# Linear attention and a routed MLP on one core: score products contracted over 32 rows of the key tile, two quarters of the heads in turn

## The reference

```python
qkv = x @ w_attn
q, k, v = jnp.split(qkv, 3, axis=-1)          # after elu+1 on q and k
def step(carry, qkv_t):
    S, z = carry
    qt, kt, vt = qkv_t
    S = S + kt[..., :, None] * vt[..., None, :]
    z = z + kt
    num = jnp.einsum('bhi,bhij->bhj', qt, S)
    den = jnp.sum(qt * z, axis=-1, keepdims=True)
    return ((S, z), num / (den + EPS))
```

## Time and profile before

| what | before |
|---|---|
| time, median of 3 runs (lowest, highest) | 357.5 us (355.8, 362.76) |
| profiled execution, first to last instruction | 339.4 us |
| PE busy | 285.0 us, 84% of the span |
| DVE busy | 241.9 us, 71% |
| ACT busy | 152.0 us, 45% |
| POOL busy | 124.8 us, 37% |
| mean granted TensorE clock | 0.934 |

### The profile page before, as it was taken

One profiled execution on the slowest core, in us unless ns is written; L12 is line 12 of the kernel. 1 busy time (PEld: TensorE's weight loads), 2 busy tenths in 40 slices (PEclk: granted clock), 3 DMA queues, 4 the chain that ended last, 5 costly groups with the idle time before them and its releaser, 6 DMA issues.

```text
span 339.4 us, 10754 instructions
## 1 busy us (share of the span) xinstructions
PE 285.0 (84%) x3847; PEld 245.5 (72%) x3847; DVE 241.9 (71%) x842; ACT 152.0 (45%) x301; POOL 124.8 (37%) x142
## 2 busy tenths in 40 slices
PE   1777989999999999999999998942129999999980
PEld 1446678688688788787787887742119999999980
DVE  4974557778778778778687787663735888988880
ACT  3378491780871871861952830000023444444430
POOL 8979000303503404305305205232311546545662
PEclk9997999999999999999999999785558999999995
DMA  7990000001000001001001001000252334333410
GB/s 212 319 302 5 3 2 2 2 3 35 34 4 37 27 0 48 16 0 63 1 0 64 0 0 66 2 34 33 82 162 70 108 90 117 93 95 97 113 38 0
DMA packets 16906, 20.19 MB, mean 59 GB/s; under 512 B 2747, under 2 KB 13117, under 8 KB 16882
## 3 DMA queue, kind: packets, MB, share of 16 engines
q1 hardware_dynamic: 13040, 12.50, 13.1%
q0 software_dynamic: 2832, 6.57, 5.6%
q10 hardware_dynamic: 1010, 0.81, 0.8%
HBM read 12.22 MB, written 8.10 MB: 60 GB/s over the span
## 4 chain that ended last, share of the span: by engine, by line
PE 63%; DVE 15%; issue 6%; ACT 4%; POOL 3%; DMA 3%; DVEq 2%; SPq 1%; POOLq 0%; ACTq 0%
PE bank L1001 18%; PE bank L1013 5%; PE bank L1138 5%; PE bank L1147 4%; PE bank L1033 4%; PE bank L1020 4%; PE bank L956 3%; DVE k_q L885 3%; PE bank L1062 3%; PE bank L979 2%; PE bank L971 2%; ACT h_t L432 2%; POOL sorted_rows L374 2%; PE bank L962 2%; PE bank L1047 2%
## 5 line engine op out<-in xcount | busy, mean ns | idle before, releaser
L374 POOL DMA_INDIRECT sorted_rows<-row_buf,slot_i x32 | 31.6, 987 | 119.7 <-DVE slot_i L777 112.4
L1001 PE MATMUL bank<-q_m,k_q 128*64 128x128 f32 x1024 | 71.9, 284 | 2.6 <-DVE probs L654 2.0
L654 DVE TENSOR_TENSOR probs<-bank,causal 128x256 f32<-128x256 f32 x128 | 51.6, 421 | 22.8 <-PE bank L1001 21.9
L1001 PEld LDWEIGHTS bank<-q_m,k_q 128*64 128x64 f32 x1024 | 56.2, 140 | 10.5 <-DVE probs L654 5.9
L396 POOL DMA_INDIRECT out_dram<-q_m,slot_token x39 | 40.8, 1047 | 44.9 <-DVE q_m L901 27.1
L1138 PE MATMUL bank<-q_m,k_q 128*128 128x128 f32 x312 | 43.0, 283 | 0.0
L1147 PE MATMUL bank<-k_q,v_m 128*128 128x128 f32 x312 | 41.5, 276 | 0.0
L1138 PEld LDWEIGHTS bank<-q_m,k_q 128*128 128x128 f32 x312 | 39.6, 199 | 0.0
L1147 PEld LDWEIGHTS bank<-k_q,v_m 128*128 128x128 f32 x312 | 38.1, 193 | 0.4 <-DVE q_m L898 0.4
L541 ACT ACTIVATE v_m<-bank 128x512 f32<-128x512 f32 x39 | 23.3, 598 | 27.2 <-PE bank L1138 27.2
L484 ACT ACTIVATE rden<-bank 128x512 f32<-128x512 f32 x8 | 4.8, 597 | 49.7 <-PE bank L987 49.6
(11 more groups left out here) (177 smaller groups left out, 510.6 us busy)
## 6 DMA issues: line engine op xcount, KB each, us to landing
v_m<-sorted_rows SPq DMA_DIRECT2D x39, 132.0 KB, 2.1
x_all<-in_L_attn_x_dram SPq DMA_DIRECT2D x16, 128.0 KB, 4.2
w_all<-in_L_ffn_W_dram SPq DMA_DIRECT2D x1, 2048.0 KB, 9.6
out_dram<-q_m,slot_token POOLq DMA_INDIRECT x39, 2.3
sorted_rows<-zeros ACTq DMA_DIRECT2D x4, 132.0 KB, 2.3
sorted_rows<-zeros SPq DMA_DIRECT2D x4, 132.0 KB, 2.5
sorted_rows<-row_buf,slot_i POOLq DMA_INDIRECT x32, 2.4
wmod_sb<-in_L_wmod_dram SPq DMA_DIRECT2D x1, 384.0 KB, 4.8
```

Of the source, the lines that this page charges most:

```text
L374: pool.indirect_dma_start(sorted_rows, bass.IndirectOffsetOnAxis(ap=slot_i[par][:, t:t + 1], axis=0), row_buf[par][:, t, :], None).then_in ...
L654: V.tensor_tensor(probs[:, s, b, q, :], score_bank[q % 2][:, 0:QUADS * L], causal[:].rearrange("p a t -> p (a t)"), ALU.mult).then_inc(pro ...
L1001: last = mm(score_bank[q % 2][L * half:L * half + L, 2 * L * n:2 * L * n + 2 * L], k_q[par][:, q, tok:tok + L], q_m[par][:, 2 * half:2 * h ...
```

## The change

The copies `k_q` are gone, with ScalarE's four activations a group, their two clears on GpSimd and their semaphore. `core_scores` takes as weights and as moving data only rows 32q to 32q+31 of `k_t` and `q_m`. It takes a pair of quarters and issues their matmuls in turn (for each chunk and half: the first quarter, then the second), where before all four matmuls of one quarter came ahead of the other's. So it waits once, for the later quarter's bank, and the two reports come on the last two matmuls. The experts' rings are buffers of their own, and counts on the semaphore `masks` fall by two.

```diff
-        k_q = [sb(f"k_q{n}", [P, QUADS, GT * P]) for n in range(2)]
+        w1_ring = sb("w1_ring", [P, WBUFS, HID])
+        w2_ring = sb("w2_ring", [P, WBUFS, HC, C])
...
-            for n in range(2):
-                nc.gpsimd.memset(k_q[n][:], 0.0).then_inc(masks, 1)
...
-                act.wait_ge(k_ready, f + 1)
-                for q in range(QUADS):
-                    rows = slice(32 * q, 32 * q + 32)
-                    last = nc.scalar.activation(k_q[par][rows, q, :], k_t[par][rows, :], ACT.Copy)
-                last.then_inc(kq_ready, 1)
...
-            def core_scores(g, par, s, b, quads=range(QUADS)):
+            def core_scores(g, par, s, b, quads):
+
                 t = 2 * b + s
                 if s == 0 and b == 0:
                     pe.wait_ge(qm_ready, g + 1)
-                    pe.wait_ge(kq_ready, g + 1)
-                for q in quads:
-
-                    pe.wait_ge(probs_ready, 16 * g + 8 * s + 4 * b + q + 1)
-                    for n in range(2):
-                        tok = t * P + n * L
-                        for half in range(2):
+                    pe.wait_ge(k_ready, g + 1)
+                pe.wait_ge(probs_ready, 16 * g + 8 * s + 4 * b + quads[1] + 1)
+                for n in range(2):
+                    tok = t * P + n * L
+                    for half in range(2):
+                        for q in quads:
+                            rows = slice(32 * q, 32 * q + 32)
                             last = mm(score_bank[q % 2][L * half:L * half + L, 2 * L * n:2 * L * n + 2 * L],
-                                      k_q[par][:, q, tok:tok + L], q_m[par][:, 2 * half:2 * half + 2, tok:tok + L],
-                                      start=True, stop=True)
-                    last.then_inc(score_mm, 1)
+                                      k_t[par][rows, tok:tok + L],
+                                      q_m[par][rows, 2 * half:2 * half + 2, tok:tok + L], start=True, stop=True)
+                            if n == 1 and half == 1:
+                                last.then_inc(score_mm, 1)
```

More of the change, by code:

```diff
@@ L179, in build @@
                                   for i in range(3))
-        w1_cur = [k_q[0][:, n, :] for n in range(WBUFS)]
-        w2_cur = [k_q[1][:, n, :].rearrange("p (k c) -> p k c", k=HC) for n in range(WBUFS)]
+        w1_cur = [w1_ring[:, n, :] for n in range(WBUFS)]
+        w2_cur = [w2_ring[:, n] for n in range(WBUFS)]
         slot_token = [sb(f"slot_token{n}", [P, 1], I32) for n in range(RING)]
@@ L205, in build @@
             sem(n) for n in ("eq_ready", "ek_ready", "q_ready", "k_ready", "qm_ready"))
-        v_ready, kn_ready, kq_ready, qz_ready, inv_ready, inv_mm, rden_ready = (
-            sem(n) for n in ("v_ready", "kn_ready", "kq_ready", "qz_ready", "inv_ready", "inv_mm", "rden_ready"))
+        v_ready, kn_ready, qz_ready, inv_ready, inv_mm, rden_ready = (
+            sem(n) for n in ("v_ready", "kn_ready", "qz_ready", "inv_ready", "inv_mm", "rden_ready"))
         score_mm, probs_ready = sem("score_mm"), sem("probs_ready")
@@ L370, in route_scatter @@
                 there = r + 1 if isinstance(r, int) else pool.to_reg(r + 1)
-                pool.wait_ge(masks, 12)
+                pool.wait_ge(masks, 10)
                 pool.wait_ge(slots_ready, there)
@@ L511, in _ @@
             front_exp(0, chain)
-            act.wait_ge(masks, 9)
+            act.wait_ge(masks, 7)
             masked_q(0, 0)
@@ L828, in _ @@
             step(0, 0, 0, chain, route=False)
-            dve.wait_ge(masks, 15)
+            dve.wait_ge(masks, 13)
             dve.wait_ge(gates_ready, 1)
@@ L1113, in _ @@
             front_inv(0)
-            core_scores(0, 0, 0, 0)
+            core_scores(0, 0, 0, 0, FIRST)
+            core_scores(0, 0, 0, 0, LAST)
             core_across(0, 0, 0)
```

## The result

The change makes the kernel slower: a median of 385.14 us (384.13 to 387.39, 4 runs) beside 359.01 us before (355.8 to 362.76, 4 runs) on the same chip, a ratio of 1.0746 with a 95% interval of 1.0667 to 1.0825. The forecast of 352.6 us, and its range up to 361, miss it by far.

A forecast was written before the change was run, and what follows sets the result against it. PE was taken to set the pace, busy 24.14 of 24.70 us a step. Start 1.0, step 0 1.1, six steps 1.7 and step 7 1.1 made 4.9 us off the 357.5 median: 352.6 us, range 347 to 361.

The forecast's parts named there:

- third rival: In the loop steps: PE's waits let the clock fall, costing 1 to 3 us a step, 358 to 370; chance 0.06.
- the walk: One loop step followed wait by wait with shorter score pairs: 0.29 us gained a step, 1.7 in six; chance 0.70.
- 10L: Score pair in each step, now needing both banks: waits some 0.9 us for VectorE's probs, gain 0.14.
- The price of a pair: Score products on PE: a pair of quarters takes 0.62 us instead of 1.09, saving 3.8 us of PE a step.
- first rival: Score pairs: rows do not overlap, a pair keeps at least its old 1.03 us; 367.9 us in all; chance 0.12.
- 01F: Score pair before inv and the projection: waits 0.7 us for both banks, starts 0.18 later, is 0.47 shorter.
- (d): Late in a step: VectorE runs in order without a wait for 6.24 us, so PE's savings meanwhile are waited away.
- VectorE as the one waited for: In the loop steps: VectorE becomes what others wait for, so only 0.29 of PE's 3.8 us a step is kept.
- The start: GpSimd's opening clears: without k_q's, VectorE's first normed x comes about 1 us earlier, worth 1.0 us (bounds 0 and 1.3).
- Step 7: Last step, with 10L at half clock: shorter score pairs gain 0.6 to 1.1 us, taken as 1.1.
- 18.1 us lie outside the span: Profiled execution of before, 339.4 us, lies 18.1 under the median of 357.5; the difference was carried over to the forecast.
- ScalarE's copies: k_q on ScalarE, 2.55 us a step: removal worth nothing, since k_n waits for PE's transposes anyway.

The follow-up runs named there:

- e6: A kernel computing nothing of the block: six streams of one kind of PE product, each after 60 full products; only clocks and product rates are reported.
- e9: A kernel computing nothing of the block: five dense streams mixing score products with four 16-column products; only the stream of 8 128-row products is reported holding 1.00.
- e3: Kernel before with one wait for both banks and only the first chunk's score products, 128 rows: 360.27 us (one run).
- e15: Kernel before with only k_q's clears moved behind GpSimd's other opening work, run again: 359.88 us, ratio 1.0034 (10 runs).
- e8: Kernel before with only k_q's clears moved behind GpSimd's other opening work: 355.44 us, ratio 0.9934.
- e2: Kernel before (128 rows, all products) with one wait for both banks and both reports at the pair's end: 377.58 us (one run).
- e1: Changed kernel without its interleaving: 32 rows, each quarter's products together and waiting for its own bank: 390.54 us.
- e14: Kernel before with one wait for both banks and only the first chunk's score products, 128 rows, run again: 363.88 us.
- e12: Kernel before with only the first chunk's score products, 128 rows, each quarter waiting for its own bank: 361.97 us, ratio 1.0129.
- e13: The changed kernel run again beside before: 384.91 us, ratio 1.0789.

## Why the prediction was wrong, and where it was right

**The step that failed is the third rival, "the clock falls in the steps".** It had 0.06, and the walk took the clock as 1.00 throughout, so the sum had nothing for its loss; the prediction did name a clock that leaves 1.00 in the loop as a sign that it was wrong. Two things were wrong in the rival. It tied the fall to PE's standing still, a wait of up to 1.0 at 10L, after the pattern of the earlier trace rows, where PE had stood still for half of the time. The changed kernel, e6 and e9 show the clock low with PE busy all the time. And it priced the fall at 1 to 3 us a step. From 63.7 to 245.3 us some 100 of the 182 are at 0.50, and a step is 30.3 us on average: 5.9 above the 24.4 of the walk, with no stop of the kind that before has. (At most half of 100 us, 50 in six steps, could be lost; PE's waits took up some of it.) The rival's bound of 370 was too low too.

The Trainium skill speaks of this. Its page "TensorE: Matmul & The Clock Gate", Part 1, has the gate follow how busy the engine has been of late. By that, the changed kernel could lose its clock only around waits; the trace doesn't agree (16.85 of 17.00 us busy at 0.50), and e6's one-quarter stream less still: PE had been busy without a gap since 135.0 when the clock fell at 156.4. The same page, Part 3, says that products in distinct row groups run at the same time; the trace agrees (0.67 a pair). It recommends such row tiles for short contractions, and the clock that they cost here stands in no row that the prediction had.

**The price of a pair** was right: 0.62 predicted, 0.67 found at full clock; 0.56 and 0.60 from its start to the next work (103.85 to 104.45). The first rival (rows don't overlap) fell, although its time (367.9) is on the side where the result lies. At half clock the pair is 1.13, where the third rival had 1.07.

**The walk through a step** was right in all its waits: 10L 0.86 us (about 0.9), 11L 0.27 (0.4), h2_t 0.43 (0.44); 01F waits 0.70 in e3 (0.7 to 0.8); VectorE's run in (d) is 6.24 in e3 as before (75.12 to 81.36); and the whole full-clock step of e3 is 24.37 (24.41). The changed kernel itself has no step that is at 1.00 throughout, so this rests on its twin with 128 rows. It means that the gain of 0.29 a step was sized rightly for a clock that the change takes away.

**VectorE as the one waited for** held only at 1.00. At 0.50 the sign turns: VectorE waits for PE, as in these rows of its timeline. (d) had it run to probs 00L without a wait, and x1 behind the projection had 1.08 of waiting:

```profile
115.67 0.76 DVE L648 TENSOR_TENSOR probs<-bank,causal 128x256 f32<-128x256 f32 x2 [0.35 <-PE bank L996]
117.48 0.23 DVE L745 TENSOR_SCALAR den<-bank 128x64 f32<-128x64 f32 x1 [1.05 <-PE bank L973]
...
126.96 0.69 DVE L679 TENSOR_TENSOR row_buf<-x_all,bank 128x512 f32<-128x512 f32 x1 [2.52 <-PE bank L1043]
```

**The start.** The clears' part was right. VectorE in the changed kernel, where the earlier trace rows had 1.38 and 0.65:

```profile
9.57 0.60 DVE L563 TENSOR_SCALAR mean<-mean 128x8 f32<-128x8 f32 x1
...
11.31 0.17 DVE L572 TENSOR_SCALAR diff<-diff 128x8 f32<-128x8 f32 x1
...
11.72 0.17 DVE L586 SCALAR_TENSOR_TENSOR shift<-mean,rstd 128x8 f32<-128x8 f32 x1
```

The shift for the first normed x is there at 11.89 instead of 13.13, 1.2 earlier. But step 0, which was to give 1.1, runs from 21 to 41.5 us and from 51.7 on at 0.50, and the first projection comes 7.0 later than in e15, 7.8 later than in e8. Either part of the change seems enough for it, by one profiled execution each: with one wait and 128 rows (e2) it came at 65.6, with 32 rows and two waits (e1) at 63.0.

**Step 7** was to give 1.1 and cost 2.6 to 2.8 against e8 and e15: the changed kernel is at 0.50 in all of it, where before had part of it at 1.00.

**"18.1 us lie outside the span"** was wrong. Each run lies 1.7 to 1.8 us above the span of its own profile (385.12 and 383.3 in the changed kernel). The profiled execution of before simply was 16 us shorter than the median; its row of steps of 24.70 is not what a usual execution on those chips has (26.6 to 29.8 from the second on). This didn't decide the error, since the same 18 us were carried over, but the walk was made in a step that the timed runs mostly don't have.

**ScalarE's copies** were rightly worth nothing: ACT is 20 us less busy (131.9 instead of 152.0), ScalarE still waits for PE's transposes ahead of k_n (19.4 us in all), and h2_t comes as in the walk.

**What is open.** Why one chip runs before in 340 us and the others in 355 to 365 isn't settled. The stops for "issue" and "remote", and the clock's falls behind some of them, are seen; what lets them happen is not. The changed kernel was not run on the fast chip, so its ratio there isn't known. The split between rows and time in the loop (17 to 20 us for the rows, from e3, e14 and the changed kernel; 2 to 4 us a step of saved work that brought nothing, from e12) comes from kernels whose clock falls at other places in each execution, and is not better than a few us. And how many rows must be at work for how much of the time was not measured.

## What to carry to other kernels

Before a contraction is cut to the rows that it needs, look at what else keeps TensorE's clock up in that stretch: wide products that look wasteful (three quarters of their rows zero) may be what holds it at full speed, and here giving them up cost 26 us where the walk had seen 5 to gain. In a loop whose engines wait for each other in a fixed order, a faster TensorE gives little (0.3 us of 3.8 here) and risks the clock of everything behind it, so check the granted clock of the stretch first, and price its loss with all of the stage's products. A step of the profiled execution can also be free of losses that most executions have. So compare the span of the profiled execution with the median before a step is walked in it.

## What was not expected of the hardware

- TensorE's granted clock falls to 0.50 and stays there with the engine busy without a gap: a dense stream of 32-row products of one quarter, and one of 16-column products, lost it 5.8 and 5.5 us after their start, and four 32-row products at once kept it when alone (372 records in 10 us) but not when mixed with narrow ones.
- Two 32x64 products at a time kept 1.00 in two quarters (17.7 us) and lost it in one quarter, at the same 52 to 53 ns a record.
- The products of `core_within`, with PE standing still for 9.8 of 24.7 us, kept 1.00 in the same kernel.
- Products with zeros in 96 of their 128 rows of weights hold the clock better than products over the 32 rows alone: 0.850 (e14) against 0.754 (e13), at equal pair times and waits.
- 32-row products of neighbouring quarters run at the same time even if each quarter's four are issued in a row (0.68 us a pair, as in turn).
- Near the start of a step engines stop for 1.0 to 3.2 us for no semaphore, on some chips in nearly every step; with the clock's falls behind some of them they make six steps of before 161.0 us (e8) and 169.5 (e15) instead of 148.2.
